# Third layer's values as three products of rounded high and low parts, the low part of x1 made on VectorE

## Chip, cores and metric

The kernel runs on one core of one Trainium2 chip. The metric is the device time of one execution in microseconds (us); less is better. Engines are named as in the profile: PE is TensorE (its weight loads are PEld), DVE is VectorE, ACT is ScalarE, POOL is GpSimd, SP is the engine that issues the DMAs.

## What is computed

A two-block graph network over 16 graphs of 512 nodes with 256 features. The first block holds two attention layers (4 heads of 128, then one of 256), the second block one attention layer; both end in a residual sum and a layer norm.

```python
def gat_layer(x, mask, W, a_src, a_dst, bias, concat):
    xl = (x @ W).reshape(B, N, H, F)
    asrc = jnp.einsum('bnhf,hf->bnh', xl, a_src)
    adst = jnp.einsum('bnhf,hf->bnh', xl, a_dst)
    e = leaky_relu(asrc[:, :, None, :] + adst[:, None, :, :], 0.2)
    attn = softmax(where(mask, e, -1e9), axis=1)
    out = jnp.einsum('bsdh,bshf->bdhf', attn, xl)
...
h  = elu(gat_layer(x, mask, W1, ..., concat=True))     # first layer, 4 heads
h  = gat_layer(h, mask, W2, ..., concat=False)         # second layer
x1 = layernorm(x + h)
Wh = x1 @ W                                            # third layer's values: the change is here
e  = leaky(Wh @ a1 [:, :, None] + Wh @ a2 [:, None, :], 0.2)
y  = layernorm(x1 + leaky(einsum('bij,bjf->bif', softmax(where(adj > 0, e, -9e15), axis=1), Wh)))
```

## The kernel before

Everything runs in fp32, with 128 nodes on the partitions, so that a graph (a batch m) is 4 blocks of nodes. Each engine has its own hand-written list of work, and semaphores tie the lists together. All lists run over slots g; a slot is one attention matrix (a unit) of one graph. Six slots make a round n = g // 6, with pos = g % 6: pos 0 is the third layer of graph n-3, pos 1 to 4 are the four heads of graph n, pos 5 is the second layer of graph n-1. So three to four graphs are in flight, and one round is one graph's worth of work. The last graphs end in a tail written out after the loop.

A unit passes through the engines in this order. DVE finds the largest score of every row (`tops`, L857) and from it the shifted column `b_t` (`shifted_targets`, L870 and L875). PE spreads it over a PSUM bank (`targets_row`, L461, bank bB). ACT applies the leaky step block by block (L693, or L697 for a third layer) and the exponential (L704, or L708). DVE cuts out the edges (`keep_edges`, L901). PE multiplies with the values (L501, L512, L522). For a head, DVE inverts the sums (`invert`, L888), ACT scales (`normalize`, L716), and the elu follows (ACT L724, DVE L882 into y1), then a transpose (PE L491) and the high and low part of y (ACT L730, DVE L894).

Values are made in PSUM tile bG, two banks of 512. For the first and second layer each product is three matmuls of operands in float32r: high times high, high times low weight, low times high weight (`values_1` L607, `values_2` L593). The low part of x is one DVE subtraction over both banks (`x_low`, L911). For the third layer both operands are plain fp32 (`values_3`, L581), one product for each k, and the profile shows two records for each fp32 product.

Around the change, in pos 3 of a round, each engine's list is:
- PE: `values_2` of blocks 2 and 3, first half of the attention of the slot before (L501), `turn_head`, `targets_row`, `turn_x1(n - 2)` (8 transposes of x1, L572, into bG), second half (L501), `sources_row` (L461, bank bA, which `tops` of the next slot needs). Pos 4 opens with `values_3(n - 2, (0, 1))`, and blocks 2 and 3 come after its `targets_row`.
- ACT: leaky steps, `values_2_out` (L752), the exponential L704, `x1_out` (two copies, L740), `elu_exp` (L724). In pos 4: leaky steps of blocks 0 and 1 (L693), `normalize` (L716), leaky steps of blocks 2 and 3, `values_3_out` (L747), L704.
- DVE: `keep_edges` (L901), then `elu` (L882). Pos 4 opens with `invert` (L888), then `tops` and `shifted_targets`.

In the tail, graphs END - 1 = 14 and END = 15 have their `turn_x1`, `x1_out`, `values_3` (L581) outside the slots. On DVE `norm_1` (L948), `tops` and `residual_2` (L957, L937, L940) stand there in written order. The weights of layers 2 and 3 are prepared once on DVE by `fold_23`.

Of the kernel before, what the change touches and what calls it, by code (L numbers as in the profile page):

```python
# [5 lines left out]
P = 128  # L6
F32 = mybir.dt.float32
F32R = mybir.dt.float32r
BF16 = mybir.dt.bfloat16
I32 = mybir.dt.int32  # L10
ALU = mybir.AluOpType
# [23 lines left out]
def gat_kernel(nc, x, adj, W1, as1, ad1, b1, W2, as2, ad2, b2, W3, a3, out):  # L35
    B, N, D = x.shape
# [3 lines left out]
    KD = D // P  # L40
    KH = HF // P
    DO = W2.shape[1]
    DX = DO + 2
# [8 lines left out]
    END = B - 1  # L52
# [24 lines left out]
    with ExitStack() as ctx:  # L77
        def sb(name, shape, dt=F32):
            return ctx.enter_context(nc.sbuf_tensor(name, shape, dt))
# [4 lines left out]
        def sem(name):  # L84
            return ctx.enter_context(nc.semaphore(name))

        bG = psum("bG", 1024)
# [4 lines left out]
        def g_bank(k):  # L92
            return bG[:, k * 512:(k + 1) * 512]
# [11 lines left out]
        w2_hi = sb("w2_hi", [P, KH, DX], F32R)  # L105
        w2_lo = sb("w2_lo", [P, KH, DX], F32R)
        w3 = sb("w3", [P, KD, DX])
        bias2 = sb("bias2", [P, DO])
        colsum = sb("colsum", [P, 2])
        neg_c = sb("neg_c", [P, 1])  # L110
# [16 lines left out]
        val3s = sb("val3s", [P, NB, DO])  # L127
        res1 = sb("res1", [P, NB, D])
        x1n = [sb(f"x1n{i}", [P, NB, D]) for i in range(2)]
        x1_t = sb("x1_t", [P, KD, N])  # L130
        act3 = sb("act3", [P, NB, D])
        res2 = sb("res2", [P, NB, D])

# [40 lines left out]
        w1_lo_ready = sem("w1_lo_ready")  # L174
        w2_hi_ready = sem("w2_hi_ready")
        w2_lo_ready = sem("w2_lo_ready")
        colsum_done = sem("colsum_done")
        colsum_out = sem("colsum_out")
        bias2_ready = sem("bias2_ready")
# [23 lines left out]
        e1_done = sem("e1_done")  # L203
        y_hi_ready = sem("y_hi_ready")
        val2_ready = sem("val2_ready")
        x1t_ready = sem("x1t_ready")
        val3_ready = sem("val3_ready")
        exp3_done = sem("exp3_done")
        act3_ready = sem("act3_ready")
# [240 lines left out]
        def _(pe):  # L450
# [3 lines left out]
            def g_wait(k):  # L454
                for signal in g_free[k] or ():
                    pe.wait_ge(*signal)
# [110 lines left out]
            def turn_x1(m):  # L567
                pe.wait_ge(x1n_done, (m + 1) * NB)
                for k in range(KD):
                    g_wait(k)  # L570
                    for b in range(NB):
                        ins = nc.tensor.transpose(g_bank(k)[:, b * P:(b + 1) * P], x1n_of[m][:, b, k * P:(k + 1) * P], ident[:])  # L572
                    ins.then_inc(x1t_turned, 1)
                    g_free[k] = ((x1t_ready, m * KD + k + 1),)

            def values_3(m, blocks):
                for b in blocks:
                    g_wait(b % 2)
                    for k in range(KD):
                        pe.wait_ge(x1t_ready, m * KD + k + 1)  # L580
                        ins = nc.tensor.matmul(g_bank(b % 2)[:, 0:DX], x1_t[:, k, b * P:(b + 1) * P], w3[:, k],  # L581
                                               start=(k == 0), stop=(k == KD - 1))
                    ins.then_inc(val3_done, 1)
                    g_free[b % 2] = ((val3_ready, m * NB + b + 1),)

# [39 lines left out]
            for g in range(FIRST, LAST + 1):  # L625
                n, pos = divmod(g, SLOTS)
                before, after, later = (units.get(g + i) for i in (-1, 1, 2))
                oldest = head_at(g - 3)
                third, second, batch = 0 <= n - 2 < B, 0 <= n - 1 < B, 0 <= n + 1 < B
                if g == 0:  # L630
                    weight_sums()
                if pos == 0 and batch:
                    turn_x(n + 1)
                if pos == 2 and batch:
                    values_1(n + 1, 1)
                if pos == 3 and second:
                    values_2(n - 1, (2, 3))
                if pos == 4 and third:
                    values_3(n - 2, (0, 1))
                if pos == 5 and batch:  # L640
                    values_1(n + 1, 2)
                if before:
                    attend(before, 0)
                if oldest:
                    turn_head(oldest)
                if after and after.row:
                    targets_row(after)
                if pos == 1 and batch:
                    if n == -1:
                        pe.wait_ge(w1_lo_ready, 1)  # L650
                        pe.wait_ge(bias1_ready, 2 * G)
                    values_1(n + 1, 0)
                if pos == 2 and second:
                    if n == 1:
                        pe.wait_ge(w2_lo_ready, 1)
                    values_2(n - 1, (0, 1))
                if pos == 3 and third:
                    turn_x1(n - 2)
                if pos == 4 and third:
                    values_3(n - 2, (2, 3))  # L660
                if pos == 5 and batch:
                    values_1(n + 1, 3)
                if before:
                    attend(before, 1)
                if later and g < LAST:
                    sources_row(later)
# [19 lines left out]
        def _(act):  # L686
# [50 lines left out]
            def x1_out(m):  # L737
                for k in range(KD):
                    act.wait_ge(x1t_turned, m * KD + k + 1)
                    nc.scalar.copy(x1_t[:, k], g_bank(k)).then_inc(x1t_ready, 1)  # L740

            def values_3_out(m, blocks):
                if m >= 2:
# [98 lines left out]
        def _(dve):  # L842
# [66 lines left out]
            def x_low(n):  # L909
                dve.wait_ge(x_hi_ready, (n + 1) * KD)  # L910
                nc.vector.tensor_tensor(x_lo[:].rearrange("p k n -> p (k n)"), bG[:],  # L911
                                        x_hi[:].rearrange("p k n -> p (k n)"), ALU.subtract).then_inc(x_lo_ready, 1)

            def invert_3(m):
                dve.wait_ge(exp3_done, (m + 1) * NB)
                if m:
                    dve.wait_ge(val3s_done, m * NB)
                nc.vector.reciprocal(z3inv[:], z3[:]).then_inc(z3inv_ready, 1)  # L918
# [94 lines left out]
            def fold_23():  # L1013
                dve.wait_ge(w23_in, 96)
                for k in range(KH):
                    fold(w2[:, k, 2:DX], att2s, w2[:, k, 0:1])
                    fold(w2[:, k, 2:DX], att2d, w2[:, k, 1:2])
                dve.wait_ge(w2_hi_ready, 1)
                nc.vector.tensor_tensor(w2_lo[:].rearrange("p k n -> p (k n)"), w2.rearrange("p k n -> p (k n)"),
                                        w2_hi[:].rearrange("p k n -> p (k n)"), ALU.subtract).then_inc(w2_lo_ready, 1)  # L1020
                for k in range(KD):
                    fold(w3[:, k, 2:DX], att3[:, 0:DO], w3[:, k, 0:1])
                    fold(w3[:, k, 2:DX], att3[:, DO:2 * DO], w3[:, k, 1:2])

            def shift_bias_2():
                dve.wait_ge(colsum_done, 1)
# [8 lines left out]
            for g in range(FIRST, LAST + 1):  # L1035
# [25 lines left out]
                    x_low(n + 1)  # L1061
                if this and this.row:
                    keep_edges(this)
                if oldest and pos != 1:
                    low_part(oldest)
                if older:
# [10 lines left out]
            tops(thirds[END - 2])  # L1077
            shifted_targets(thirds[END - 2])
            norm_1(END - 1)
            tops(final_second)  # L1080
            shifted_targets(final_second)
            invert_3(END - 2)
# [10 lines left out]
            invert_3(END - 1)  # L1093
            norm_1(END)
            residual_2(END - 2, range(NB))
            tops_by_targets(thirds[END])
            norm_2(END - 2, range(NB))
            for j in range(NB):
# [32 lines left out]
```

## Time and profile before

| what | value |
|---|---|
| time, 3 runs | 967.58 us median, 967.22 to 968.35 |
| time of the profiled execution | 967.98 us |
| its span, first to last instruction | 965.8 us |
| PE busy / PEld busy | 91% / 85% |
| DVE / ACT / POOL busy | 78% / 71% / 26% |
| granted TensorE clock, mean | 0.98 |
| chain that ended last | PE 36%, DVE 30%, ACT 25%, issue 8% |
| L581, third layer's values | 256 matmul records, 62.5 us busy |
| L911, low part of x | 16 instructions, 19.5 us busy |

Busy time of PE adds up matmuls that overlap; what one record costs the engine is the distance from start to start, which the chain of waits gives as the length of a piece divided by its count. The timeline gives the profiled duration of an instruction; on DVE and ACT the next one can start a little before that is over.

### The profile page before, as it was taken

Reading aid. Unit: us, or ns where it says so; the run is one execution under the profiler, and the core shown is the slowest. Engines: PE = TensorE matmul, PEld = TensorE weight load, DVE = VectorE, ACT = ScalarE, POOL = GpSimd, SP = SyncE. Lnnn points to the kernel's source line nnn. Section 1 sums busy time; section 2 is a strip of 40 time slices with the busy share of each in tenths; the row PEclk is TensorE's granted clock in tenths of the full one; section 3 lists DMA queues with packets and bytes.
Section 4 is the critical chain, followed back from the end, with each engine's and each line's share of the span. In section 5 each row is a group of like instructions: output and inputs, shape, how many; then the busy total and the mean of one; then the engine's idle time right before and its main releaser. Section 6 shows DMA issues by size and latency. Waiting matters only on the chain.

```text
span 965.8 us, 17300 instructions
## 1 busy us (share of the span) xinstructions
PE 881.6 (91%) x6220; PEld 819.6 (85%) x6220; DVE 751.0 (78%) x1906; ACT 686.8 (71%) x1272; POOL 255.4 (26%) x242
## 2 busy tenths in 40 slices
PE   5786889999999999999999999999999999998675
PEld 4676879998999989898999989898998989897564
DVE  5757687888788888878888888878888888875446
ACT  2466758787786877878686877778686877875533
POOL 1001001124242313324232422424231332424112
PEclk9898999999999999999999999999999999999988
DMA  6403030302104030301203030311203010000001
GB/s 202 120 1 88 1 88 2 88 1 58 54 24 87 3 108 1 110 2 41 71 22 89 1 109 2 74 37 29 81 22 89 2 44 1 24 1 22 1 0 66
DMA packets 62732, 45.03 MB, mean 47 GB/s; under 512 B 35765, under 2 KB 54325, under 8 KB 62649
## 3 DMA queue, kind: packets, MB, share of 16 engines
q1 hardware_dynamic: 62648, 43.93, 16.1%
q8 instruction: 51, 0.84, 0.4%
q14 instruction: 33, 0.26, 0.1%
HBM read 27.14 MB, written 8.39 MB: 37 GB/s over the span
## 4 chain that ended last, share of the span: by engine, by line
PE 36%; DVE 30%; ACT 25%; issue 8%; POOL 0%; DMA 0%; SPq 0%; POOLq 0%; DVEq 0%; ACTq 0%
DVE junk L857 9%; PE bU L501 6%; PE bG L607 6%; PE bG L593 6%; PE bU L522 6%; ACT att L704 6%; ACT att L693 6%; ACT x L716 5%; DVE att L901 3%; DVE y_lo L894 3%; PE bB L461 3%; DVE low L870 3%; DVE y L882 3%; ACT att L708 2%; ACT att L697 2%
## 5 line engine op out<-in xcount | busy, mean ns | idle before, releaser
L857 DVE CUSTOM_DVE_ANT_0 junk<-mask_t,bA,val 128x512 bf16<-128x512 bf16 x320 | 219.7, 742 | 42.4 <-PE bA L461 38.8
L501 PE MATMUL bU<-val,att 128*128 128x129 f32 x2048 | 249.6, 275 | 3.2 <-DVE att L901 3.2
L501 PEld LDWEIGHTS bU<-val,att 128*128 128x128 f32 x2048 | 241.4, 192 | 5.7 <-issue 3.4
L901 DVE SCALAR_TENSOR_TENSOR att<-mask_n,att 128x2048 f32<-128x2048 bf16 x79 | 181.0, 2292 | 82.1 <-ACT att L704 81.7
L693 ACT ACTIVATE att<-bB,val 128x512 f32<-128x512 f32 x320 | 202.9, 708 | 1.3 <-PE bB L461 1.3
L704 ACT ACTIVATE att<-att 128x2048 f32<-128x2048 f32 x79 | 153.4, 1941 | 0.7
L512 PE MATMUL bU<-val,att 128*128 128x257 f32 x480 | 111.2, 385 | 3.5 <-DVE att L901 3.5
L756 ACT COPY val<-bG 128x524 f32<-128x524 f32 x64 | 38.7, 605 | 106.1 <-PE bG L607 106.1
L522 PE MATMUL bU<-val3s,att 128*128 128x256 f32 x480 | 109.2, 381 | 0.6
L716 ACT ACTIVATE x<-bU,zinv 128x128 f32<-128x128 f32 x256 | 73.4, 375 | 47.9 <-DVE zinv L888 47.7
L512 PEld LDWEIGHTS bU<-val,att 128*128 128x128 f32 x480 | 89.8, 192 | 16.1 <-DVE att L901 3.7
L522 PEld LDWEIGHTS bU<-val3s,att 128*128 128x128 f32 x480 | 89.1, 190 | 14.4 <-issue 3.2
L372 POOL TENSOR_SCALAR var_eps<-moments 128x4 f32<-128x4 f32 x29 | 5.7, 195 | 352.4 <-DVE moments L940 352.3
L381 POOL TENSOR_SCALAR act<-res,moments,rstd 128x256 f32<-128x256 f32 x52 | 86.4, 1672 | 1.5
L593 PE MATMUL bG<-w_hi,y_hi 128*128 128x258 f32 x256 | 76.1, 297 | 5.2 <-ACT val L752 5.2
L406 POOL TENSOR_SCALAR val3s<-val,z3inv 128x256 f32<-128x256 f32 x64 | 40.7, 653 | 135.1 <-DVE z3inv L918 107.7
L461 PE MATMUL bB<-ident,b_t 128*128 128x128 f32 x320 | 51.1, 284 | 27.2 <-DVE b_t L875 27.0
L607 PE MATMUL bG<-w_hi,x_hi 128*128 128x262 f32 x256 | 75.5, 295 | 0.0
L607 PE MATMUL bG<-w_lo,x_hi 128*128 128x262 f32 x256 | 75.2, 294 | 0.0
L607 PE MATMUL bG<-w_hi,x_lo 128*128 128x262 f32 x256 | 75.1, 293 | 0.0
L593 PE MATMUL bG<-w_hi,y_lo 128*128 128x258 f32 x256 | 73.0, 285 | 0.0
L593 PE MATMUL bG<-w_lo,y_hi 128*128 128x258 f32 x256 | 73.0, 285 | 0.0
(111 smaller groups left out, 1620.8 us busy)
## 6 DMA issues: line engine op xcount, KB each, us to landing
adj_in<-in_adj_dram SPq DMA_DIRECT2D x16, 1024.0 KB, 5.9
x_in<-in_x_dram SPq DMA_DIRECT2D x16, 512.0 KB, 6.8
out_dram<-act SPq DMA_DIRECT2D x14, 512.0 KB, 2.9
mask_t<-mask_n SPq DMA_TRANSPOSE x64, 2.5
att<-in_L_gnn_W_dram SPq DMA_DIRECT2D x4, 128.0 KB, 3.3
att<-in_L_gnn_W_dram SPq DMA_DIRECT2D x1, 512.0 KB, 7.1
out_dram<-x_in SPq DMA_DIRECT2D x1, 512.0 KB, 2.9
out_dram<-x_in SPq DMA_DIRECT2D x2, 256.0 KB, 2.1
```

What stands on the lines that cost most here:

```text
L381: nc.gpsimd.tensor_scalar(act3[:, b], res2[:, b], moments[:, 1, b, 0:1], rstd[:, 1, b:b + 1], ALU.subtract, ALU.mult).then_inc(y_out_done, 1)
L461: ins = nc.tensor.transpose(bank[:, b * P:(b + 1) * P], column(b).to_broadcast([P, P]), ident[:])
L501: ins = nc.tensor.matmul(to[:, (d % 2) * FX:(d % 2 + 1) * FX], p[:, s, d * P:(d + 1) * P], val1[u.batch % 2][:, s, u.index // 2, values], ...
L512: ins = nc.tensor.matmul(to[:, 0:DO + 1], p[:, s, d * P:(d + 1) * P], val2[:, s, 2:DX + 1], start=(s == 0), stop=(s == NB - 1))
L522: ins = nc.tensor.matmul(to[:, d * DO:(d + 1) * DO], p[:, j, (2 * i + d) * P:(2 * i + d + 1) * P], val3s[:, j], start=(j == 0), stop=(j == ...
L593: ins = nc.tensor.matmul(g_bank(b % 2)[:, 0:DX], left[:, k, nodes], right[:, k], start=(k == 0 and i == 0), stop=(k == KH - 1 and i == 2))
L607: ins = nc.tensor.matmul(to, left[:, k, nodes], right[:, k, g], start=False, stop=(k == KD - 1 and i == 2))
L693: nc.scalar.activation(p[:, b], bB[:], ACT.Prelu, bias=a_col(u, b), alpha=SLOPE)\
L704: nc.scalar.activation(flat(p), flat(p), ACT.Exp).then_inc(exp_done, 1)
L716: nc.scalar.activation(x1[u.h % 2][:, d * P:(d + 1) * P], bU[u.use[d // 2] % 4][:, (d % 2) * FX:(d % 2) * FX + F], ACT.Copy, scale=zinv[u. ...
L857: nc.vector.tensor_tensor_reduce(junk[:, b] if u.row else att[u.slot % 3][:, b], mask_t[u.batch % 4][:, b], bA[:], 1.0, a_col(u, b) if u.r ...
L901: nc.vector.scalar_tensor_tensor(flat(p), mask_n[u.batch % 3][:, 0:NB * N], BIG, flat(p), ALU.add, ALU.min)\
```

## The change

The third layer's weights are split once, in `fold_23`, into a rounded high part and a low part. x1's transpose leaves PSUM as a rounded high part (two ACT copies, as before, now into float32r), and DVE subtracts it from PSUM for the low part: one instruction over both banks, placed in pos 3 between `keep_edges` and `elu`, and in the tail at two places. `values_3` then does three float32r matmuls for each k instead of one in fp32, and waits for the low part ahead of its first product. The PSUM banks are given free only when both parts are out.

```diff
+        w3_hi = sb("w3_hi", [P, KD, DX], F32R)
+        w3_lo = sb("w3_lo", [P, KD, DX], F32R)
...
-        x1_t = sb("x1_t", [P, KD, N])
+        x1_hi = sb("x1_hi", [P, KD, N], F32R)
+        x1_lo = sb("x1_lo", [P, KD, N], F32R)
...
-                    g_free[k] = ((x1t_ready, m * KD + k + 1),)
+                    g_free[k] = ((x1_hi_ready, m * KD + k + 1), (x1_lo_ready, m + 1))
...
             def values_3(m, blocks):
                 for b in blocks:
                     g_wait(b % 2)
+                    pe.wait_ge(x1_lo_ready, m + 1)
                     for k in range(KD):
-                        pe.wait_ge(x1t_ready, m * KD + k + 1)
-                        ins = nc.tensor.matmul(g_bank(b % 2)[:, 0:DX], x1_t[:, k, b * P:(b + 1) * P], w3[:, k],
-                                               start=(k == 0), stop=(k == KD - 1))
+                        for i, (left, right) in enumerate(((x1_hi, w3_hi), (x1_hi, w3_lo), (x1_lo, w3_hi))):
+                            ins = nc.tensor.matmul(g_bank(b % 2)[:, 0:DX], left[:, k, b * P:(b + 1) * P], right[:, k],
+                                                   start=(k == 0 and i == 0), stop=(k == KD - 1 and i == 2))
...
                 if pos == 4 and third:
+                    if n == 2:
+                        pe.wait_ge(w3_lo_ready, 1)
                     values_3(n - 2, (0, 1))
...
-                    nc.scalar.copy(x1_t[:, k], g_bank(k)).then_inc(x1t_ready, 1)
+                    nc.scalar.copy(x1_hi[:, k], g_bank(k)).then_inc(x1_hi_ready, 1)
...
+            def x1_low(m):
+                dve.wait_ge(x1_hi_ready, (m + 1) * KD)
+                nc.vector.tensor_tensor(x1_lo[:].rearrange("p k n -> p (k n)"), bG[:],
+                                        x1_hi[:].rearrange("p k n -> p (k n)"), ALU.subtract).then_inc(x1_lo_ready, 1)
...
+                nc.vector.tensor_copy(w3_hi[:], w3[:]).then_inc(w3_hi_ready, 1)
+                dve.wait_ge(w3_hi_ready, 1)
+                nc.vector.tensor_tensor(w3_lo[:].rearrange("p k n -> p (k n)"), w3[:].rearrange("p k n -> p (k n)"),
+                                        w3_hi[:].rearrange("p k n -> p (k n)"), ALU.subtract).then_inc(w3_lo_ready, 1)
...
                 if this and this.row:
                     keep_edges(this)
+                if pos == 3 and 0 <= n - 2 < B:
+                    x1_low(n - 2)
                 if oldest and pos != 1:
                     low_part(oldest)
...
             norm_1(END - 1)
+            x1_low(END - 1)
             tops(final_second)
...
             residual_2(END - 2, range(NB))
+            x1_low(END)
             tops_by_targets(thirds[END])
```

## Rows read from the trace of the kernel before

**Rows 1.** The page's first part: busy time and share of the span.

```profile
PE 881.6 (91%) x6220; PEld 819.6 (85%) x6220; DVE 751.0 (78%) x1906; ACT 686.8 (71%) x1272; POOL 255.4 (26%) x242
```

**Rows 2.** Busy time by stretch, two rounds; then clock, DMA share, GB/s.

```profile
407.00:462.00 55.00, 53.44 (x390) 50.24 (x390) 45.84 (x114) 42.49 (x79) 17.61 (x15) 1.00 0.16 50
462.00:517.00 55.00, 53.45 (x390) 50.24 (x390) 45.85 (x114) 42.50 (x79) 17.61 (x15) 1.00 0.17 50
```

**Rows 3.** Chain of waits over one round: start, length, what, count.

```profile
424.89 0.17 DVE b_t L875
...
459.76 0.65 PE bB L461 x4
...
474.59 0.45 PE bA L461 x4
...
479.87 0.17 DVE b_t L875
```

**Rows 4.** Chain of waits from pos 3 into pos 5.

```profile
484.06 0.70 ACT x L716 x3
...
488.64 0.51 DVE att L901
...
490.85 0.68 DVE y_lo L894
...
493.72 0.13 DVE zinv L888 x2
```

**Rows 5.** Timeline of DVE around the new instruction's place: start, duration, instruction, [idle before].

```profile
480.18 2.29 DVE L901 SCALAR_TENSOR_TENSOR att<-mask_n,att 128x2048 f32<-128x2048 bf16 x1 [0.15 <-ACT att L704]
482.94 0.69 DVE L882 SCALAR_TENSOR_TENSOR y<-e,x 128x512 f32<-128x512 f32 x1 [0.46 <-ACT e L724]
483.55 0.23 DVE L888 RECIPROCAL zinv<-bU 128x2 f32<-128x2 f32 x2
```

**Rows 6.** Timeline of ACT, same place.

```profile
481.21 1.08 ACT L740 COPY x_t<-bG 128x512 f32<-128x512 f32 x2 [1.06 <-PE bG L572]
...
483.94 1.16 ACT L716 ACTIVATE x<-bU,zinv 128x128 f32<-128x128 f32 x4
```

**Rows 7.** Timeline of DVE, the low part of x and its neighbours.

```profile
34.42 1.22 DVE L911 TENSOR_TENSOR x_lo<-bG,x_hi 128x1024 fp32r<-128x1024 f32 x1
35.55 0.74 DVE L857 CUSTOM_DVE_ANT_0 junk<-mask_t,bA,val 128x512 bf16<-128x512 bf16 x1
```

**Rows 8.** Chain of waits, round 2: the first third-layer values and a second-layer burst.

```profile
147.10 2.90 PE bG L593 x24
...
155.32 1.75 PE bG L581 x8
```

**Rows 9.** Timeline of PE, the first half of the third layer's values.

```profile
483.67 1.91 PE L581 MATMUL bG<-w,x_t 128*128 128x258 f32 x8
```

**Rows 10.** Timeline of DVE before the first `tops`.

```profile
29.62 0.75 DVE L857 CUSTOM_DVE_ANT_0 junk<-mask_t,bA,val 128x512 bf16<-128x512 bf16 x1 [2.26 <-issue]
```

**Rows 11.** Groups by line: busy us, mean ns of one | idle before.

```profile
L957 DVE TENSOR_TENSOR res<-act,x1n 128x512 f32<-128x512 f32 x2 | 1.3, 680 | 0.0
```

**Rows 12.** Timeline at the tail: the first product of graph 15, last copy, last DVE step.

```profile
935.41 5.08 PE L581 MATMUL bG<-w,x_t 128*128 128x258 f32 x16
935.53 0.59 ACT L740 COPY x_t<-bG 128x512 f32<-128x512 f32 x1 [0.27 <-PE bG L572]
935.91 0.36 DVE L940 BATCH_NORM_AGGREGATE moments<-stats 128x2 f32<-128x6 f32 x4
```

**Rows 13.** Chain of waits in the tail: a second-layer burst, then graph 15's values.

```profile
900.58 4.68 PE bG L593 x24
...
935.50 5.01 PE bG L581 x16
```

**Rows 14.** Busy time by stretch in the tail; the clock is the third number from the end.

```profile
935.50:938.00 2.50, 2.50 (x6) 1.94 (x7) 0.77 (x6) 0.96 (x2) 1.20 (x2) 0.50 0.00 0
938.00:940.60 2.60, 2.50 (x11) 1.77 (x10) 0.00 (x0) 0.82 (x3) 0.00 (x0) 0.97 0.00 0
```

More of the change, by code:

```diff
@@ L176, in gat_kernel @@
         w2_lo_ready = sem("w2_lo_ready")
+        w3_hi_ready = sem("w3_hi_ready")
+        w3_lo_ready = sem("w3_lo_ready")
         colsum_done = sem("colsum_done")
@@ L205, in gat_kernel @@
         val2_ready = sem("val2_ready")
-        x1t_ready = sem("x1t_ready")
+        x1_hi_ready = sem("x1_hi_ready")
+        x1_lo_ready = sem("x1_lo_ready")
         val3_ready = sem("val3_ready")
```

## The prediction

> **What bounds the kernel now.** I read four views in this order: busy shares, rounds, chain, and then the three timelines at the place of the edit. The shares [rows 1] name PE first, 91% against 78% for DVE and 71% for ACT. By round the picture is the same but closer: a round takes 55.00 us and PE is busy in 53.44 of them, DVE in 45.84, ACT in 42.49 [rows 2]. That PE is nearly full doesn't yet say that its work sets the period: 1.56 us in every round are idle, and something closes them. The chain of waits tells what. It meets the same DVE step, `b_t` of pos 3, at 424.89 and at 479.87, so it is a loop of 54.98 us, which is the whole period [rows 3]. In that loop PE is on the path in one long stretch only, from 459.76 to the end of the spread at 475.04, pos 1 and 2 [rows 3]. From pos 4 on the loop runs on ACT and DVE: the scaling, the leaky steps and the exponential, `keep_edges`, and DVE's steps up to `zinv`, after which ACT scales again [rows 4]. **L581, the work that becomes cheaper, is not in the loop of a steady round at all.** It is on the path in the first round that has a third layer, and in the tail [rows 8, 13]. The reader should see two facts: PE is almost full, and yet the edit puts work into the stretch where DVE and ACT set the pace.
>
> **What the change takes from PE.** 8 records of L581 take 1.75 us of the chain, and a round has 16, so 3.50 us. The new form has 24 float32r matmuls of the same 258 columns, which L593 does in 2.90 us [rows 8]. PE gains 0.60 us a round, 0.30 at each half. In a steady round this shortens no step of the loop, so I cost it at nothing. What covers it is the wait that is there anyway: PE's next steps hang on `b_t` and on ACT.
>
> **What it adds to PE: a wait.** `values_3` (0, 1) opens pos 4 at 483.67 [rows 9], and now it needs x1_lo. That is ready at 482.39 + 1.22 = 483.61 (next part), about when its weight load starts anyhow, so the wait costs 0.1 us at most. Queued behind it on PE are the first half of an attention (L501), a transpose and the spread of `b_t` for the slot after. The shorter burst (0.30) more than pays for the wait. The spread then waits for `b_t`, which comes 0.6 later (next part); PE has gained 0.2 by then, so it idles a little, and the leaky step that reads the spread stands behind a whole exponential in ACT's list. I cost the wait at nothing; without that cover it would be 0.1 a round.
>
> **What it adds to DVE.** One subtraction over 1024 columns from PSUM, which is what L911 does: 1.22 us long, and the next instruction starts 1.13 after it [rows 7]. It is 16 x 1.13 = 18 us in all, 14 of them in the loop (rounds 2 to 15) and 2 in the tail. Now its place. `keep_edges` starts at 480.18, and behind L901 DVE is free 2.21 later, as the next L901 shows, whose follower starts at 490.85 behind 488.64 [rows 4], so at 482.39. x1_hi must be ready: ACT's two copies run from 481.21 to 482.29 [rows 6], just in time. Then the subtraction holds DVE until 483.52. `elu` (L882) started at 482.94, since it waited 0.46 for the exponential [rows 5]; it now starts 0.58 later. `invert` was at 483.55 and goes to 484.13, and with its 0.23 the inverse is out at 484.36 [rows 5]. ACT's scaling L716 started at 483.94 [rows 6], held by ACT's own queue, so it now starts at 484.36: **0.42 late**. Of 1.13 us, 0.55 fell into DVE's wait for the exponential and 0.16 into ACT's slack, and 0.42 are left.
>
> **Where these 0.42 go.** L716 is in the loop [rows 4], and each later step of the loop was released by the one ahead of it, so all of them move: the exponential, `keep_edges` at 488.64, `zinv` at 493.72, the next round's `b_t`, then PE's long stretch. Nothing in that stretch got shorter. So a steady round takes 55.4 us. The ends for the size: 0.3 if ACT's copies and DVE overlap a little better, 0.55 if the high part is out 0.1 late. Round 2 is different: PE is on the path there [rows 8], DVE has no idle time ahead of `elu`, and I estimate that the whole 1.1 us enters, is partly taken up by slack and comes out as 0.5. Sum of the loop: 13 x 0.42 + 0.5 = 6.0 us.
>
> **One-time weights.** The cast and the subtraction of 516 columns are added to `fold_23`. No row shows that cast; a subtraction of 512 columns takes 0.68 [rows 11], so both are between 0.7 (cast for nothing) and 1.4 us. DVE stands idle for 2.26 us right behind [rows 10], and PE needs w3_lo first at 155. Cost nothing; if that idle time were gone, 1.4 at most.
>
> **The tail.** Graph 14: `x1_low` comes ahead of `tops` of the final second layer, which moves 1.3 us, but the path there runs over ACT's exponentials and the second half of L581, and the shorter burst gives back what the wait takes. I cost it at nothing, 0.3 either way. Graph 15 is different, since the path goes through its values [rows 13]. Before, PE began at 935.41 behind the first copy. Now it needs both copies (936.12), DVE's aggregates ahead of it (936.2), and the subtraction: 936.2 + 1.22 = 937.4, so it starts 2.0 us later [rows 12]. The burst took 5.01 us for 16 records [rows 13], for the granted clock was 0.50 until about 938, the 1.2 GHz level, and 0.97 after that [rows 14]. The new burst of 24 at full clock takes 2.90 [rows 8]; after a long idle stretch of PE the same 24 took 4.68 [rows 13]. Here PE idles 2 us more ahead of the burst, so I take 4.68: 937.4 + 4.7 = 942.1 against 940.5, which is +1.6. The ends are -0.2 (2.4 GHz throughout) and +2.7 (1.2 GHz throughout, twice 2.90). I take +1.5.
>
> **Sum.** 6.0 + 1.5 = 7.5 us on the profiled execution's 967.98, 975.5. That execution is 0.4 above the median of 967.58, so I forecast 975.1 us.
>
> **Rivals.**
> - *PE sets the pace after all (faster).* PE's 53.44 of 55.00 speak for it; the loop that leaves L581 out speaks against it. The mechanism is that PE's queue reaches pos 5 and pos 0 earlier by 0.60 and releases ACT and DVE there; it decides if DVE's added delay has at least 0.4 us of slack up to the next spread. Then 14 x 0.60 = 8.4 fall away, and with +1.5 in the tail the time is 960.7 us. The Trainium skill (Perfetto Trace Analysis, Identifying the Most-Contended Engine) says to find the engine with the highest occupancy, for TensorE by its weight loads' busy share, and to optimize it first; by that rule this edit works on the right engine and should pay. I give it 0.09, as the chain, not the share, has had the say in every round looked at.
> - *The delay is absorbed.* Slack that the chain doesn't show takes up 0.42 a round, and only the tail is left: 967.6 to 969.1. Against it: the loop is 54.98 of 55.00. Chance 0.08.
> - *The whole subtraction is paid.* If x1's high part comes late each round, or `elu` starts a second wait, 1.13 a round enter: 14 x 1.13 + 1.5 = 17.3, 984.9 us. Against it stand the 0.46 idle ahead of L882. Chance 0.07.
> - *The matmuls don't get cheaper.* Were the new product no faster than 3.50 us a round, the loop would hardly change, since it has no L581, and the time would stay near 975 to 977. This is within the forecast.
>
> **How the numbers follow.** The forecast, 971.5 to 978.0 with its bounds (0.3 to 0.55 a round is 4.2 to 7.7; the tail -0.2 to +2.7), has 0.76. To hold 8 in 10 the range reaches half way into the absorbed case and a little past the upper bound: 968.3 to 978.5. One measurement of this kernel can tell about 0.2% (1.9 us) from no change. Faster by more has 0.10 (the first rival), within it 0.08 (the second), slower 0.82.
>
> **What would show it.** The rounds should be 55.4 us apart. PE's busy time in a round should fall by about 0.6, DVE's rise by 1.2. L882 in pos 3 should have no idle time before it and start about 3.3 us after L901; L716 in pos 4 should wait for `zinv` some 0.4. L581's successor should not stand in the steady chain, and x1_lo should. In the tail PE should wait about 2 us for x1_lo. A period of 55.0 or less, or x1_lo absent from the chain, makes the prediction wrong.

## The result, and the profile after

The changed kernel takes 975.12 us (median of 5 runs, 974.88 to 978.87), the kernel before 967.58 us beside it (5 runs, 966.48 to 971.58). The ratio is 1.007, with a 95% interval of 1.0048 to 1.0093: slower by 0.7%. The forecast was 975.1 us. The profiled execution of the changed kernel took 974.88 us with a span of 972.7 us; the one of before had a span of 965.8 us. The spans differ by 6.9 us, the medians by 7.5 us.

First the busy shares of the changed kernel, from its page, to be read against [rows 1]:

```profile
PE 876.2 (90%) x6348; PEld 818.5 (84%) x6348; DVE 769.0 (79%) x1924; ACT 686.0 (71%) x1272; POOL 254.9 (26%) x242
```

PE is busy for 5.4 us less and DVE for 18.0 us more. The second number is mainly the 16 subtractions (16 times 1.13 us); the first is smaller than the forecast, 0.60 us in each of 16 rounds. By these shares alone the change looks harmless, since both engines stay below full.

Then one round by stretch, in the columns of [rows 2]:

```profile
407.00:462.50 55.50, 53.23 (x399) 50.22 (x399) 46.91 (x115) 42.40 (x79) 17.57 (x15) 1.00 0.17 49
```

PE falls from 53.44 to 53.23 and DVE rises from 45.84 to 46.91. The length of a round is read more exactly from an instruction that occurs once in each. I take POOL's addition of the bias. Two of its rows on the timeline of POOL, ten rounds apart, in the changed kernel:

```profile
257.30 2.36 POOL L404 TENSOR_TENSOR x_in<-x_in,bias 128x1024 f32<-128x1024 f32 x1
...
811.41 2.36 POOL L404 TENSOR_TENSOR x_in<-x_in,bias 128x1024 f32<-128x1024 f32 x1
```

These are 554.11 us for ten rounds. In the kernel before, the same rows stand at 257.48 and 807.47, 549.99 us apart. A round takes 55.41 us, and took 55.00 us. All rounds given below are measured so.

Now the place of the edit. This is the timeline of DVE (start, duration, instruction), to be read against [rows 5]:

```profile
426.23 2.29 DVE L910 SCALAR_TENSOR_TENSOR att<-mask_n,att 128x2048 f32<-128x2048 bf16 x1
428.44 1.22 DVE L925 TENSOR_TENSOR x_lo<-bG,x_hi 128x1024 fp32r<-128x1024 f32 x1
429.58 0.68 DVE L891 SCALAR_TENSOR_TENSOR y<-e,x 128x512 f32<-128x512 f32 x1
430.17 0.23 DVE L897 RECIPROCAL zinv<-bU 128x2 f32<-128x2 f32 x2
```

and the scaling that it releases, from the timeline of ACT, against [rows 6]:

```profile
430.44 1.14 ACT L725 ACTIVATE x<-bU,zinv 128x128 f32<-128x128 f32 x4 [0.30 <-DVE zinv L897]
```

`elu` starts 3.35 us after `keep_edges` (2.76 before) and has no idle time ahead of it. The scaling starts 4.21 us after `keep_edges`, 3.76 before, so 0.45 us late, and for 0.30 us of that ACT stands waiting for `zinv`. And this is the chain of waits (start, length, what) at the same place:

```profile
421.10 2.89 PE bG L600 x24
...
424.02 0.37 ACT val L761
424.39 1.82 ACT att L713
...
426.23 2.20 DVE att L910
...
428.44 1.22 DVE x_lo L925
429.66 0.60 DVE y L891
430.26 0.16 DVE zinv L897 x2
...
430.44 0.39 ACT x L725 x2
```

The subtraction is a link of the chain in each steady round. In [rows 3] this stretch hung on `b_t`; now the exponential in ACT (L713) and `keep_edges` lead to it. Why the way in has changed comes out of the last pair of experiments.

Where the 6.9 us of the spans went, by POOL's additions and the end of the span:

| stretch | before | after | difference | forecast |
|---|---|---|---|---|
| start, to the addition in round 2 | 146.99 | 145.48 | -1.51 | 0 |
| round 2 | 55.45 | 56.40 | +0.95 | +0.5 |
| 11 steady rounds | 605.03 | 609.53 | +4.50 | +4.6 |
| the round behind them | 50.02 | 50.42 | +0.40 | +0.4 |
| the next, 15 | 25.69 | 26.67 | +0.98 | +0.4 |
| the tail | 82.62 | 84.20 | +1.58 | +1.5 |
| span | 965.8 | 972.7 | +6.9 | +7.5 |

(The graphs' last rounds have fewer slots, so their distances are shorter.) The first line is scatter of the start: kernels whose start is the same as the changed one's have that mark between 145.48 and 149.23 us. It can't be laid to the change, and it also blurs the total of each run, as does the tail, whose line is one pair of executions (see the tail of graph 15 below); differences of under 3 us between two kernels below are read from the rounds.

### The profile page after: what moved, and what is told of

It reads as the page before. It is cut to its first block, busy times and chain, and to the rows that moved or that the text cites. A ratio compares the mean times of both kernels' runs of the same rounds, so it can differ in the third digit from the quotient of the medians.

```text
span 972.7 us, 17575 instructions
## 1 busy us (share of the span) xinstructions
PE 876.2 (90%) x6348; PEld 818.5 (84%) x6348; DVE 769.0 (79%) x1924; ACT 686.0 (71%) x1272; POOL 254.9 (26%) x242
## 4 chain that ended last, share of the span: by engine, by line
PE 36%; DVE 30%; ACT 25%; issue 7%; POOL 0%; DMA 0%; SPq 0%; POOLq 0%; DVEq 0%; ACTq 0%
PE bG L600 9%; ACT att L713 9%; DVE att L910 6%; PE bU L528 6%; PE bG L614 6%; PE bU L507 6%; DVE junk L866 5%; ACT x L725 5%; ACT att L702 4%; DVE y L891 4%; DVE y_lo L903 3%; DVE stats L951 2%; ACT att L717 2%; PE bB L467 2%; ACT att L706 2%
## 5 line engine op out<-in xcount | busy, mean ns | idle before, releaser
L713 ACT ACTIVATE att<-att 128x2048 f32<-128x2048 f32 x79 | 152.9, 1936 | 0.7
```

The source lines that it names most:

```text
L713: nc.scalar.activation(flat(p), flat(p), ACT.Exp).then_inc(exp_done, 1)
```

## The experiments

Two theories were to be told apart. **Mine:** the subtraction lies in a loop through ACT and DVE, PE's shorter bursts lie outside it, and so the two halves of the change cost +0.42 and 0. **The rival:** PE sets the pace, or would if it were let, and the delay has another reason. Later a third question came up: what a steady round hides that rounds 2 and 15 do not.

**1. The elu taken out from behind the subtraction.** In pos 3 `elu` is put behind the inverse:

```
-                if older:
+                if older and pos != 3:
                     elu(older)
 ...
                     invert(older)
+                if pos == 4 and head_at(g - 3):
+                    elu(head_at(g - 3))
```

> The changed kernel with one order altered on DVE: the elu of pos 3 stands behind the inverse that opens pos 4, not ahead of it. Theory (the subtraction costs a steady round 0.45 us because it pushes the inverse, and with it ACT's scaling, past the moment at which ACT is free): the inverse starts 3.34 us after keep_edges, is out at about 3.6, and ACT is free at 3.76, so the 0.45 vanish and the rounds are 55.0 us apart again; about 6 us come back, 969 to 970 us, with the tail's 1.6 us still lost. Rival (the subtraction costs what it costs because DVE's list is full, or because PE waits for x1_lo): moving a step behind another on the same engine changes nothing, rounds 55.4, 975 us.

Measured: a round of 54.99 us, and 971.18 us in all (ratio to before 1.0032, 1.0013 to 1.0051). The timeline of DVE:

```profile
425.88 2.29 DVE L910 SCALAR_TENSOR_TENSOR att<-mask_n,att 128x2048 f32<-128x2048 bf16 x1
...
429.22 0.23 DVE L897 RECIPROCAL zinv<-bU 128x2 f32<-128x2 f32 x2
429.36 0.67 DVE L891 SCALAR_TENSOR_TENSOR y<-e,x 128x512 f32<-128x512 f32 x1
```

The inverse is out 0.6 us earlier, the scaling starts 3.75 us after `keep_edges` as it did before (3.76), and the round is that of before, with the subtraction, its wait and the new products all in place. The delay of `zinv` is therefore the whole cost in a steady round. Of the total less came back than the forecast 6 us. The rounds of the profiled executions give back 6.3 us (rounds 2 and 15 stay 0.34 and 0.38 above before), but against the changed kernel's the start is 1.9 us longer, and the tail 1.8 us longer with the same code.

**2. One half of the change at a time.** The subtraction alone, with the old products (its output isn't used):

```
+            def x1_low(m):
+                dve.wait_ge(x1t_ready, (m + 1) * KD)
+                nc.vector.tensor_tensor(x1_lo[...], bG[:], x1_t[...], ALU.subtract).then_inc(x1_lo_ready, 1)
 ...
                     keep_edges(this)
+                if pos == 3 and 0 <= n - 2 < B:
+                    x1_low(n - 2)
```

> The kernel before, with DVE's part of the change alone: the third layer's values stay one fp32 product from an unrounded x1, and DVE does the subtraction at the same three places, into a tile that nothing reads; PE waits for it only where the banks are reused. Theory (in a steady round PE's saving is worth nothing): rounds 55.4 apart as in the changed kernel, and 975.5 to 977.5 us, a little above it, since the tail's burst and round 2 keep the longer fp32 products. Rival (PE's saving of 0.60 a round does count, and the change lost more on DVE than it won on PE): rounds 56.0 apart, 983 us.

The products alone; here x1_low is neither computed nor waited for, and the third product reads the high part of x1 and the low part of the weights instead:

```
-                if pos == 3 and 0 <= n - 2 < B:
-                    x1_low(n - 2)
 ...
-    ((x1_hi, w3_hi), (x1_hi, w3_lo), (x1_lo, w3_hi))
+    ((x1_hi, w3_hi), (x1_hi, w3_lo), (x1_hi, w3_lo))
```

> The changed kernel with PE's part alone: three float32r products for each k, but the low part of x1 isn't made and the third product takes the high part in its place, so the output lacks the low part's share. Theory: PE is 0.60 us a round shorter and the rounds stay 55.0 apart, because the loop has no third-layer values in it; only round 2 (0.5) and the tail's burst (1.0) give something, 965.5 to 967 us. Rival (PE's load sets the period): rounds 54.4 apart, 958 to 960 us.

Measured: the subtraction alone 55.43 us a round (977.38 us, ratio 1.0109, 1.0076 to 1.0141); the products alone 54.98 us a round (966.60 us, ratio 0.9992, 0.9975 to 1.0008). The sum of the two halves is the whole (+0.43 and -0.02 against +0.41).

**3. Twice the subtraction, and half of it.** Twice, one behind the other:

```
+                nc.vector.tensor_tensor(x1_lo[...], bG[:], x1_hi[...], ALU.subtract).then_inc(x1_lo_once, 1)
+                dve.wait_ge(x1_lo_once, m + 1)
                 nc.vector.tensor_tensor(x1_lo[...], bG[:], x1_hi[...], ALU.subtract).then_inc(x1_lo_ready, 1)
```

> The changed kernel with the subtraction done twice in a row, the second behind the first's end. Theory (0.68 us of cover is used up by the first, the rest is paid one for one): a second subtraction of 1.22 with its wait is paid in full, rounds 56.6 to 56.7 apart, some 16 us more than the changed kernel, with 1.2 more in each tail step. Rival (DVE has about 8 us of idle time a round, and delays are shared between lists): less than 0.8 more a round, rounds below 56.2.

Half: only the first 512 columns; the third product of the second half is that of the high part again, as in the products alone:

```
-    nc.vector.tensor_tensor(x1_lo[...], bG[:], x1_hi[...], ALU.subtract)
+    nc.vector.tensor_tensor(x1_lo[:, 0], bG[:, 0:N], x1_hi[:, 0], ALU.subtract)
```

> The changed kernel with the low part made for the first half of x1's features only; the second half's third product takes other operands, so that share is missing from the output. The subtraction is over 512 columns, 0.68 us long, and DVE goes on some 0.6 after its start. Theory (the first 0.68 us on DVE in this place are covered: 0.55 by the wait for the exponential, 0.13 by ACT's own queue): nothing is left to pay, rounds 55.0 apart, 969 to 971 us with the tail. Rival (the cost is proportional, 0.41 for 1024 columns): rounds 55.2.

Measured: 56.73 us a round for twice (one run, 999.34 us), 54.98 us for half (971.65 us, ratio 1.003, 1.0013 to 1.0047). The timelines of DVE, twice and then half:

```profile
491.86 1.22 DVE L926 TENSOR_TENSOR x_lo<-bG,x_hi 128x1024 fp32r<-128x1024 f32 x1
493.11 1.23 DVE L929 TENSOR_TENSOR x_lo<-bG,x_hi 128x1024 fp32r<-128x1024 f32 x1
494.25 0.68 DVE L892 SCALAR_TENSOR_TENSOR y<-e,x 128x512 f32<-128x512 f32 x1
```

```profile
429.91 0.68 DVE L925 TENSOR_TENSOR x_lo<-bG,x_hi 128x512 fp32r<-128x512 f32 x1
430.51 0.68 DVE L891 SCALAR_TENSOR_TENSOR y<-e,x 128x512 f32<-128x512 f32 x1
```

The half holds DVE for 0.60 us and costs nothing; the whole holds it for 1.14 us and costs 0.41; the second copy adds 1.25 us on DVE and 1.32 to the round. That is a cover of about 0.7 us and full price behind it: 0.60 is less than 0.7, 1.14 exceeds it by 0.4, and of anything more nothing is hidden. The prediction's cover was 0.55 + 0.16 = 0.71. The total for twice is 24.2 us above the changed kernel, where some 18 were expected. The rounds hold 18.3 of them; the other 6.0 lie in the tail, where the two added subtractions take 2.5 and two bursts of PE ran slower in that one execution (5.53 and 5.50 us, 4.48 and 3.23 in the changed kernel).

**4. Another step of the same loop moved.** If DVE's work in this loop is the price, then taking other DVE work out must pay at the same rate, in both kernels. The statistics of pos 4 (L951 and L954) go behind the inverse of pos 5:

```
-                if pos == 4 and 0 <= n - 3 < B:
-                    norm_stats(n - 3, 1, ...)
 ...
                     invert(older)
+                if pos == 5 and 0 <= n - 3 < B:
+                    norm_stats(n - 3, 1, ...)
```

In the changed kernel:

> The changed kernel with DVE's four statistics and four aggregates of the second norm (1.59 us, pos 4) moved behind the inverse that opens pos 5. Theory (the loop runs through DVE's list in pos 4, and whatever stands ahead of the inverse there is paid in full): the inverse waits for PE's attention instead, and a round takes 53.8 to 54.2 us, PE's own load of 53.2 being the floor; 955 to 959 us. Rival (PE's or ACT's list is next to the bound, so that little comes back): rounds 55.0 to 55.3, 970 us or more.

In the kernel before:

> The kernel before with the four statistics and four aggregates of the second norm moved behind the inverse that opens pos 5, as it was done to the changed kernel, whose rounds went from 55.44 to 53.87. Theory (the loop gives back 1.59 in both, until PE's own list is the floor): the loop alone would give 53.4, but PE was busy 53.44 of each round and idle steps remain, so the rounds are 53.5 to 53.9 apart and the time is 949 to 954 us; the rest of the change would still cost 5 us or more. Rival (the second norm's statistics were holding back something that only the fp32 kernel has in its path): rounds above 54.4, no better than the changed kernel with the same move.

In the changed kernel's chain of waits these steps were links:

```profile
438.61 1.31 DVE stats L951 x4
439.92 0.28 DVE moments L954 x4
440.20 0.13 DVE zinv L897 x2
```

and with them moved the chain goes straight on:

```profile
435.05 0.60 DVE y L891
435.64 0.16 DVE zinv L897 x2
```

Measured: 53.88 us a round in the changed kernel (959.95 us, ratio 0.9908, 0.9877 to 0.9939) and 53.51 in the one before (950.49 us, ratio 0.9808, 0.9787 to 0.9828). 1.59 us of chain taken away gave 1.53 and 1.49 us a round. The place of these two DVE steps is worth over three times what the change costs a round, and no engine has less work by it. The kernel before is at another limit with this: its chain of waits now passes both bursts of L581 (1.75 us each), and in the next experiment it gains nothing more (53.51 again).

**5. When PE's saving counts.** On top of that, `elu` is put behind the inverse in three slots:

```
-                if older:
+                if older and pos not in (3, 4, 5):
                     elu(older)
 ...
                     invert(older)
+                if pos in (4, 5, 0) and head_at(g - 3):
+                    elu(head_at(g - 3))
```

In the changed kernel:

> The changed kernel with the statistics moved, and with the elu of pos 3, 4 and 5 behind the inverse that opens the next slot. Theory: DVE's part of the loop shrinks by 0.45 in pos 3 and by 0.6 at each of the next two places, until PE's own list is the floor; PE was busy 53.2 a round, so 53.1 to 53.5 us a round and 948 to 953 us. Rival (y1 comes too late for PE's transposes, which takes back what the inverse gains): rounds 53.8 or more, 958 us.

In the kernel before:

> The kernel before with the same two moves. Here the loop no longer bounds and PE does, so PE's 0.60 a round should show: rounds 53.6 to 54.0 apart against 53.1 to 53.5 for the changed kernel with the same moves, and 950 to 955 us, 2 to 7 us slower than that kernel once the tail's 1.6 us are counted. Rival (PE isn't the floor in either): the same rounds in both, and this one faster by the tail's 1.6 us.

Measured: 53.25 us a round in the changed kernel (944.92 us, ratio 0.9748, 0.9728 to 0.9768), 53.51 in the one before (946.18 us, ratio 0.9769, 0.9738 to 0.98). Here the sign has turned: the round with the change is the shorter one, by 0.26 us. Busy time of a round, changed and then before, both with this order:

```profile
410.91:464.16 53.25, 52.71 (x398) 50.10 (x398) 46.69 (x115) 42.20 (x79) 18.07 (x17) 1.00 0.17 50
```

```profile
411.74:465.26 53.52, 53.01 (x391) 50.23 (x390) 45.77 (x114) 42.21 (x79) 18.09 (x17) 1.00 0.17 51
```

PE is idle for only 0.5 us a round in both, and the chain of waits now runs through the third layer's values. The bursts, changed and then before:

```profile
417.29 1.63 PE bG L588 x12
...
421.71 1.44 PE bG L588 x12
```

```profile
422.54 1.75 PE bG L581 x8
```

The other burst of before has the same 1.75 us. 3.07 us against 3.50 us: 0.43 us a round are saved on PE, and 0.26 of them arrive in the round. Another 0.12 goes where PE now waits for `b_t` between the bursts: the spread takes 0.56 us of the chain there and 0.44 before. So the prediction's first rival is not wrong in itself; it needs the loop through DVE out of the way first. In time the two kernels can't be told apart here (intervals 0.9728 to 0.9768 and 0.9738 to 0.98); the rounds can. Three expectations were missed: the round of the kernel before is under the 53.6 given for it, and both totals are under their ranges, in part because the addition in round 2 stands at 142.0 and 141.9 us in these two kernels, and at 145.5 and 147.0 in the two kernels that they are made from.

The Trainium skill (Perfetto Trace Analysis, Identifying the Most-Contended Engine) says to optimize the engine with the highest occupancy first, TensorE being judged by the busy share of its weight loads. With PE at 91% of the span, and its weight loads at 85%, that rule gave nothing for the products alone (54.98 against 55.00 us), and work moved on DVE, at 78%, gave 1.49. The rule comes true in this experiment, where the delay on DVE no longer closes the round and PE is busy in 99% of it.

**6. What a steady round hides.** Rounds 2 and 15 paid 0.95 and 0.98, not 0.41. On the timelines of the kernel before, a step ahead of the edit is oddly long:

```profile
477.44 2.37 POOL L398 TENSOR_TENSOR x_in<-x_in,bias 128x1024 f32<-128x1024 f32 x1
477.87 1.97 DVE L870 SCALAR_TENSOR_TENSOR low<-top,val 128x4 f32<-128x4 f32 x1
479.87 0.16 DVE L875 SCALAR_TENSOR_TENSOR b_t<-top,low 128x4 f32<-128x4 f32 x1
```

`low` handles 4 columns. It lasts 1.97 us and ends at 479.84, with POOL's addition at 479.81; `b_t`, of the same kind and size, takes 0.16. In rounds 2 and 15 of the same kernel the addition is over when `low` starts (146.99 + 2.40 against 149.94, and 857.49 + 2.40 against 860.12), and there `low` takes 0.17 us. The collision occurs in rounds 3 to 14, each time with 1.75 to 1.99 us for `low`. To test it, POOL's addition is held back until a later inverse:

```
+                    if n < B:
+                        pool.wait_ge(zinv_ready, (H * n + 2) * 2)
                     add_bias_2(n - 1)
```

In the kernel before:

> The kernel before with one wait added on POOL: the addition of the second bias to x (2.37 us) starts with the inverse of pos 4, not right behind the diagonal's step. In the traces DVE's little step ahead of the shifted column of pos 3 lasts 1.97 us, and not 0.17, while this addition runs. Theory (the two exclude each other, and the loop passes through it): the step is 0.17 long again, the x1 copy comes 0.9 to 1.1 earlier, the inverse then bounds ACT's scaling, and a round takes 54.2 to 54.5 us; 957 to 961 us. Rival (the step is long for another reason, or another list takes over at once): 54.9 or more.

In the changed kernel:

> The changed kernel with the same wait on POOL. Its loop does not pass the shifted column of pos 3 but keep_edges, which waits for ACT's exponential, the subtraction and the elu. Theory: nothing comes back, rounds 55.3 to 55.5, 974 to 976 us, so that against the kernel before with the same wait the subtraction costs 1.1 us a round, its full length. Rival (POOL's addition costs both kernels the same): 54.7, 965 us.

Measured: 54.42 us a round in the kernel before (959.78 us, ratio 0.9912, 0.9892 to 0.9931), and 55.40 in the changed one (976.65 us, ratio 1.0088, 1.0064 to 1.0112). From the first one's timelines:

```profile
474.07 0.17 DVE L872 SCALAR_TENSOR_TENSOR low<-top,val 128x4 f32<-128x4 f32 x1
...
479.51 2.36 POOL L398 TENSOR_TENSOR x_in<-x_in,bias 128x1024 f32<-128x1024 f32 x1 [5.83 <-DVE zinv L890]
```

```profile
476.39 2.29 DVE L903 SCALAR_TENSOR_TENSOR att<-mask_n,att 128x2048 f32<-128x2048 bf16 x1 [1.96 <-ACT att L706]
478.60 0.68 DVE L884 SCALAR_TENSOR_TENSOR y<-e,x 128x512 f32<-128x512 f32 x1
```

No `low` in this run lasts over 0.17 us. The round gains 0.58, and `elu` follows `keep_edges` after 2.21 us with no idle time, where [rows 5] had 0.46 of it. This explains the account of the rounds. In the kernel before, the held-up `low` makes `b_t` late, so the spread, ACT's copies and its exponential are late, and DVE waits for that exponential ahead of `elu`. The subtraction fills this wait: 1.13 - 0.55 - 0.16 = 0.42. Where `low` isn't held up, there is no such wait to fill, and the subtraction costs 1.13 less ACT's slack of about 0.1: the scaling starts 4.21 us after `keep_edges` and not 3.17, which is 1.04 late. Measured are 55.40 - 54.42 = 0.98 a round, and 0.95 and 0.98 in rounds 2 and 15. The earlier runs bear it out: in rounds 2 and 15 half the subtraction cost 0.39 and 0.42 (in a steady round nothing), twice the subtraction 2.24 and 2.25, the subtraction alone 1.07 and 0.99, and the products alone -0.09 and -0.05. It also explains why the chain of the changed kernel no longer passes `b_t`: its loop goes through the exponential and `keep_edges` into the subtraction, and there moving POOL's addition is worth nothing (55.40 against 55.41).

**7. All of it together.** The orders of experiments 5 and 6 in the changed kernel:

> The changed kernel with the statistics, the three elus and POOL's addition all later, the candidate for the fastest. The loop of the kernel with the first two (53.25 a round) passes the 1.97 us step. Theory: that step drops out, PE's own list of 52.7 busy becomes the floor, rounds 52.8 to 53.0, 939 to 943 us. Rival (the addition now collides with something else on DVE, or PE was the floor already): rounds 53.2 or more, 945 us.

Measured: 53.23 us a round, 944.24 us (ratio 0.9754, 0.9736 to 0.9771). `low` is short in it, and yet the round is that of experiment 5 (53.25), and not 52.8 to 53.0 as expected. The collision of `low` costs nothing in this order, though PE still stands idle for 0.67 us of the round:

```profile
400.00:453.20 53.20, 52.53 (x398) 50.04 (x398) 44.97 (x117) 42.33 (x79) 18.50 (x15) 1.00 0.18 51
```

In its chain a loop with the subtraction is left, which ends in a burst of PE and not in the inverse:

```profile
413.41 2.29 DVE att L912
415.70 1.15 DVE x_lo L927
...
416.98 1.72 PE bG L590 x12
```

This and the kernel of experiment 5 are the fastest that I have, 2.5% below the kernel before; between the two there is no difference that can be measured.

## The prediction, point by point

**The steady round: right, in size and in mechanism.** 0.42 was forecast and 0.41 measured; the terms hold one by one. `elu` 0.58 later: measured 0.59 (3.35 against 2.76). The scaling 0.42 late: 0.45. The cover of 0.71: between 0.60 and 1.14 by experiment 3, and 0.7 by the price of what lies beyond it. PE's new wait for the low part, forecast at 0.1 at most, is small too: its burst starts 3.58 us after `keep_edges`, 3.49 before. Experiment 1 shows that nothing else of the change costs a steady round anything.

**PE's saving is worth nothing: right. Its size was taken too high.** Forecast were 0.60 us a round from 2.90 us for 24 matmuls. That row is one unbroken burst, and the new form runs in two bursts of 12. The timeline of PE shows how a burst begins and how it goes on:

```profile
429.81 0.36 PE L588 MATMUL bG<-w_hi,x_hi 128*128 128x258 f32 x1
430.00 0.29 PE L588 MATMUL bG<-w_lo,x_hi 128*128 128x258 f32 x1
...
431.34 1.95 PE L507 MATMUL bU<-val,att 128*128 128x129 f32 x16
```

The first matmul takes 0.19 us to the next start, the other eleven 0.12 each, so a burst takes 1.53 us where it took 1.75. That saves 0.44 a round. PE's busy time fell by 0.2 and not by 0.6. The term was multiplied by nothing, so the sum didn't suffer; in experiment 5, where it counts, 0.6 would have misled.

**Round 2: +0.5 forecast, +0.95 measured; and round 15, taken as a steady one, +0.98.** This is the step that failed. I had written that the whole 1.1 us enters round 2 and that slack takes half. The runs show that nothing of that kind takes it: the cover of a steady round is a wait that POOL's addition causes, and these two rounds don't have it. The price is 1.13 less the 0.1 or so that ACT has to spare. It was 1.0 us short over both.

**The graph 14 stretch: 0 forecast.** The chain there has the subtraction in it, unlike before, and the burst behind it is the new one:

```profile
912.15 1.24 DVE x_lo L925
...
913.52 3.23 PE bG L588 x24
```

So the path there was not the one forecast, over ACT's exponentials. The stretch as a whole came out 0.3 us shorter, but 0.2 of that is the second-layer burst ahead of it (4.48 us, 4.68 before), which the change doesn't touch and which takes 5.53 in the kernel of experiment 1. What the change costs there stays open.

**The tail of graph 15: +1.5 forecast, and 1.58 for the whole tail. The wait was right; the match in size is partly luck.** This is the chain of waits and the timeline of PE, against [rows 12, 13]:

```profile
941.33 1.12 DVE x_lo L925
...
942.59 4.84 PE bG L588 x24
```

```profile
942.59 0.55 PE L588 MATMUL bG<-w_hi,x_hi 128*128 128x258 f32 x1 [2.03 <-DVE x_lo L925]
```

PE waits for 2.03 us (2.0 forecast), and the burst took 4.84 us (4.68 forecast), since the granted clock was again at the 1.2 GHz level behind the idle time, and between the levels after that:

```profile
942.50:945.00 2.50, 2.41 (x11) 2.44 (x12) 0.00 (x0) 0.37 (x1) 0.28 (x1) 0.50 0.00 0
945.00:947.50 2.50, 2.42 (x15) 2.20 (x13) 0.00 (x0) 0.79 (x3) 0.00 (x0) 0.71 0.00 0
```

Of graph 15 alone the cost is 2.03 us of waiting less the 0.17 us by which the burst is shorter than the 5.01 us of before, 1.9 us; with the 0.3 gained in the stretch ahead this makes the 1.6. The new products take 2.90 us at full clock, but PE isn't there in this place, and before the change it was there only in the later half of the burst [rows 14]. The products alone, without the added wait, took 5.11 us here against 5.01, so in the tail the runs show no saving of the new form on PE. The term came near because its burst was taken from a row with an idle stretch ahead of it, and also by chance: behind the same wait of 2.02 to 2.03 us the burst took 5.51 us in experiments 1 and 4 (granted clock 0.50 all through in the first), 5.43 in experiment 5 and 5.37 in experiment 6. The whole tail took 85.96 us in experiment 1 and 84.20 in the changed kernel, with the same code. Pairs of kernels with and without the change differ in the tail by 2.03 us (experiment 4), 1.52 (experiment 5) and 0.01 (experiment 6).

**The one-time weights: 0, not settled.** The cast (0.43 us) and the subtraction (0.70 us) fall into DVE's idle time of [rows 10]; `tops` starts directly behind, at 27.91, where it was at 29.62 before:

```profile
27.24 0.70 DVE L1040 TENSOR_TENSOR w_lo<-w,w_hi 128x516 fp32r<-128x516 f32 x1
27.91 0.75 DVE L866 CUSTOM_DVE_ANT_0 junk<-mask_t,bA,val 128x512 bf16<-128x512 bf16 x1
```

With no idle time left, up to 1.1 us could have entered, but the start scatters by more than that from kernel to kernel, and no experiment here separates it.

**The rivals.** PE as the pacemaker fell with the products alone, the absorbed delay with the round of 55.41, and so did the whole subtraction paid, though nearly that case (0.98 of 1.13) is what happens in the two rounds without the held-up `low`. The matmuls did get cheaper. That the total met 975.1 so closely is chance: the five runs lie between 974.88 and 978.87 us, and in the profiled execution 1.0 us too little for rounds 2 and 15 stands against a start 1.5 us early.

## What to carry to other kernels

Find the loop that closes a round before counting what an engine saves: 0.44 us off the engine that is busy for 97% of the round bought nothing, and 1.6 us moved out of the loop on a less busy one bought 1.5. Cost an added instruction as its time less the waits that it fills, and ask what causes each such wait, since the cover goes where its cause is missing (0.41 against 0.98 us here), and beyond the cover the price is full. Take the duration of a burst from a row of the same length and with the same idle time ahead of it, and give it a range: the same 24 matmuls behind the same wait took from 4.84 to 5.51 us.

## What the runs showed of the hardware

A DVE instruction of 4 columns lasts 1.97 us and not 0.17 when it meets POOL's addition of 1024 columns (2.37 us), and it ends 0.03 us behind it. With the addition moved, the same instruction takes at most 0.17 us in the whole run, and the round is 0.58 us shorter. The Trainium skill (SBUF — State Buffer, SBUF: two separate sides) describes an exclusive lock on the port pair that DVE and GpSimd share, held for a whole instruction, which a DVE operation with two SBUF inputs takes against a GpSimd operation that reads SBUF. The traces agree: `low` has two SBUF inputs, and it waited out the whole addition. `tops` (L857), which reads the PSUM bank bA, takes 0.74 to 0.75 us beside a POOL operation as it does elsewhere. And the kernel of experiment 7 shows the reverse order. There `elu` starts first, with two SBUF inputs, and POOL's addition behind it lasts 2.74 us and not 2.36:

```profile
416.89 0.67 DVE L893 SCALAR_TENSOR_TENSOR y<-e,x 128x512 f32<-128x512 f32 x1
```

```profile
417.06 2.74 POOL L404 TENSOR_TENSOR x_in<-x_in,bias 128x1024 f32<-128x1024 f32 x1 [6.31 <-DVE zinv L899]
```

Such a wait is counted as busy time of the engine that waits, so it doesn't show as idle; one sees it only in an instruction that is too long for its shape.

At a granted clock of 1.00 the float32r matmul of 258 columns takes 0.12 us to the next start in a burst and 0.19 as the first of one, and two records of the old form take 0.22 each. Three products in place of one are therefore cheaper on PE by 13%, not by the 17% that the long burst gave.
